# Cross-attention: Q and K pieces moved to the first visits, ctx in two halves, stack loads ahead of packing and stores, maxima three visits ahead

## The chip, the cores and the metric

The kernel runs on one core of a Trainium2 chip. TensorE multiplies into PSUM, VectorE (DVE), ScalarE (ACT) and GpSimd (POOL) compute, SyncE (SP) issues most DMAs; POOL and ACT issue some. The metric is the device time of one execution in microseconds, the lower the better. The three runs of the kernel before have a median of 2131.28 us (2120.72 to 2146.82).

## The reference

`x` is [8, 512, 320], the context [8, 1601, 512]; there are 20 heads of 16. The last 8 tokens of the context are four dummy and four image-prompt tokens with own weights and a mask from boxes; the first 1593 are text.

```python
q = split_heads(x @ w_q)                       # 20 heads of 16
k = split_heads(text @ w_k); v = split_heads(text @ w_v)
out_text = softmax(q k^T / 4) v
k_ip = split_heads(ip @ w_k_ip); v_ip = split_heads(ip @ w_v_ip)
out_ip = softmax(q k_ip^T / 4 + mask_ip) v_ip
out = (out_text + out_ip) @ w_out + b_out + x  # all in float32
```

## The kernel before

**Batches, groups, visits.** There are 8 batches of 5 groups; a group is four heads, so 40 groups run one after another. A group's scores are 12 tiles of 128 keys for each of four heads plus a half tile for two pairs: 50 exp tiles. They are taken in 17 **visits** (0 to 16) of three tiles (two in the last). In each visit TensorE multiplies three *max tiles* for a later group into the three banks of `max_bank` (`max_tile`, L602), three *exp tiles* of this group into `exp_bank` (`exp_tile`, L638, L642), at most one P·V tile (`pv_tile`, L654; visits 1, 5, 9 and 13 have none) and at most one *turn* of work from `work_plan`. ACT takes the exponentials (L815), VectorE the maxima of the three max banks in one reduction (L904).

**Maxima ahead.** A softmax needs the row maximum first. Round r of 17 reduces three banks; round 0 is the short tail of the keys (`max_rest`, 16 small matmuls, L613) and the first to touch the group's stack. `round_at` puts round v + LEAD in visit v, with LEAD = 2: in visit 15 starts round 0 of the group two after the one whose exps run, and the rounds of the next group end in visit 14. Then `negative_parts` on VectorE, a transposing matmul at visit NEG_AT = 15 (L536), a copy by ACT, and two DMAs from ACT's queue (L798) bring the negated maxima as extra rows into `q_stack`. The first exp tile of the next group waits for them (`neg_loaded`, L720).

**Stacks.** Scores run in float32r, on values split into a high and a low part. Projections K (`k_piece`, L480, two halves of four steps) and Q (`q_piece`, L491, three steps) go to `work_bank`; ACT copies them out, POOL splits them (`split_k`, `split_q`), SP stores them to scratch (`store_k`, `store_q`) and loads them back stacked (`load_k`, 12 DMAs, L364 and L367; `load_q`, 6 DMAs, L377) into a ring of three slots. Group n's stack comes from Q made in group n - 2 and K made in group n - 3.

**Other pieces.** V (`v_piece`, L513, L519; four steps, twelve tiles and a tail for each batch), OUT (`out_piece`, L529; the output projection of the batch before, four steps for each of four row tiles, in group 1), IP (the image tokens' scores), WA, WB, TA, TB (small). A piece is spread over visits by `put(group, piece, steps, (visit, steps), ...)`. `work_bank` is one bank, so a piece begins when the one before is copied out (`work_empty`). In group 2 VectorE does the mask softmax in visits 4 and 12.

**SP's order in a group.** `normalise` (sums, reciprocals, `r_wide`; L387 to L392) for the group before; in group 1 then `store_out` of the batch before (L405) and the pack; in others the pack (`o_sum` into `o_t`, four DMAs, L401); then `slot_free`, `load_k`, `store_q`, `load_q`; then `store_k`. In group 0 the residual `xres` (L437) is loaded first. ACT's `o_copy` in visit 0 waits for the pack before. POOL issues the next batch's ctx (`load_ctx`, L1082) behind the split of the last K piece of the batch.

Of the kernel before, what the change touches and what calls it, by code (L numbers as in the profile page):

```python
# [38 lines left out]
HEADS_IN_TURN = (0, 2, 1, 3)  # L39
# [11 lines left out]
LEAD = 2  # L51
# [9 lines left out]
V_EARLY = 8  # L61
PV_AT = {0: FULL, 2: 0, 3: 1, 4: 2, 6: 3, 7: 4, 8: 5, 10: 6, 11: 7, 12: 8, 14: 9, 15: 10, 16: 11}
NEG_AT = 15


def work_plan(first, last):
# [12 lines left out]
    put(0, ("V", 8), 4, (1, 4))  # L79
    put(0, ("V", 9), 4, (2, 2), (3, 2))  # L80
    put(0, ("V", 10), 4, (4, 2), (5, 2))
    put(0, ("V", 11), 4, (6, 2), (7, 2))
    put(0, ("V", 12), 4, (8, 1), (9, 3))
    put(0, ("K", 3, 0), 4, (10, 1), (11, 1), (12, 2))
    put(0, ("K", 3, 1), 4, (13, 3), (14, 1))
    put(0, ("IP", 2), 1, (16, 1))
    if not first:
        put(1, ("OUT", 0), 4, (0, 1), (1, 3))
        put(1, ("OUT", 1), 4, (2, 1), (3, 1), (4, 2))
        put(1, ("OUT", 2), 4, (5, 4))  # L90
        put(1, ("OUT", 3), 4, (6, 1), (7, 1), (8, 2))
    put(1, ("Q", 3), 3, (9, 3))
    put(1, ("K", 4, 0), 4, (10, 1), (11, 1), (12, 2))
    put(1, ("K", 4, 1), 4, (13, 3), (14, 1))
# [7 lines left out]
    if not last:  # L102
        put(2, ("V", 0), 4, (3, 1), (4, 1), (5, 2))
        put(2, ("K", 5, 0), 4, (6, 1), (7, 1), (8, 2))
        put(2, ("V", 1), 4, (9, 3), (10, 1))
        put(2, ("K", 5, 1), 4, (11, 1), (12, 1), (13, 2))
        put(3, ("Q", 5), 3, (0, 3))
        put(3, ("V", 2), 4, (1, 3), (2, 1))
        put(3, ("V", 3), 4, (3, 1), (4, 1), (5, 2))
        put(3, ("K", 6, 0), 4, (6, 1), (7, 1), (8, 2))  # L110
        put(3, ("V", 4), 4, (9, 3), (10, 1))
        put(3, ("K", 6, 1), 4, (11, 1), (12, 1), (13, 2))
        put(3, ("IP", 5), 1, (14, 1))
        put(4, ("Q", 6), 3, (0, 3))
        put(4, ("V", 5), 4, (1, 3), (2, 1))
        put(4, ("V", 6), 4, (3, 1), (4, 1), (5, 2))
        put(4, ("K", 7, 0), 4, (6, 1), (7, 1), (8, 2))
        put(4, ("V", 7), 4, (9, 3), (10, 1))
        put(4, ("K", 7, 1), 4, (11, 1), (12, 1), (13, 2))
        put(4, ("IP", 6), 1, (14, 1))  # L120
# [12 lines left out]
SCALE_AT = (1, 0, 1, 1, 1)  # L133
# [24 lines left out]
PRO_PLAN += [(("V", 6), ALL, 1), (("NEG", 0), ALL, 0), (("V", 7), ALL, 2)]  # L158
# [28 lines left out]
def cross_attention(nc, x, x_t, ctx_t, ctx_ip_t, boxes, grid, own_k_rows, own_v_rows, ident, w_q, w_k, w_v, w_k_ip, w_v_ip,  # L187
# [6 lines left out]
    with ctx:  # L194
# [142 lines left out]
        def _(sp):  # L337
# [94 lines left out]
            def body(b, first, last):  # L432
                number = lambda piece: work_number(b, piece, first, last)
                for g in range(NG):
                    group_no = b * NG + g
                    if g == 0 and not first:
                        sp.dma_start(xres[:, :, :], x[b - 1].rearrange("(t p) d -> p t d", p=128))\  # L437
                          .then_inc(residual_loaded, 16)
                    if group_no:
                        normalise(group_no - 1)  # L440
                    if g == 1:
                        if not first:
                            for t in range(QT):
                                store_out(b - 1, t, number(("OUT", t)))
                        pack(group_no - 1, 0, None if first else number(("OUT", QT - 1)))
                    elif group_no:
                        pack(group_no - 1, (g - 1) % NG, None)
# [5 lines left out]
                    if g == 2 and not first:  # L453
                        sp.wait_ge(out_stored, b * QT * 16)
                    if group_no + 3 < B * NG:
                        store_k(group_no + 3)

# [11 lines left out]
        def _(pe):  # L469
# [69 lines left out]
            def work(b, piece, turn, first, last):  # L539
# [12 lines left out]
                elif kind == "V":  # L552
                    if piece[1] == 0 and begins(turn):
                        pe.wait_ge(ctx_next_loaded, (b + 1) * CT * 16)
# [487 lines left out]
        def _(pool):  # L1042
# [37 lines left out]
            def load_ctx(b):  # L1080
                for c in range(CT):
                    pool.dma_start(ctxt[:, c, :], ctx_t[b, c * 128:(c + 1) * 128, :]).then_inc(ctx_next_loaded, 16)  # L1082
# [96 lines left out]
```

## Time and profile before

| | |
|---|---|
| median of three runs | 2131.28 us (2120.72 to 2146.82) |
| profiled execution | 2132.55 us, span 2130.7 us |
| mean granted TensorE clock | 0.952 |
| busy | PE 1921.7, DVE 1291.3, ACT 1203.1, POOL 301.9 us |
| maximum reductions (L904) | 672, 1726 ns each |
| chain that ended last | PE 60%, DVE 22%, DMA 9% |

The matmul rows overlap and their ends are modelled, so PE's busy share is not a measure of a full TensorE. In timeline rows the first number is the start, the second the duration; the bracket tells how long the engine had been idle before, and what ended that. One reduction L904 belongs to each visit, so the distance of their starts is the length of a visit.

### The profile page before, as it was taken

The numbers are of one execution on the slowest core, as the hardware profiler recorded it, in microseconds if no ns is written. First come the engines' busy times: TensorE is split into PE (matmuls) and PEld (weight loads), VectorE is DVE, ScalarE is ACT, GpSimd is POOL, SyncE is SP. The second block draws the span as 40 slices with busy tenths as digits, with TensorE's granted clock in tenths as the row PEclk, the third lists the DMA queues.
The fourth block names the chain that finished last, engine by engine and source line by source line (L and its number), as shares of the span: only waits on it lengthen the run. The fifth ranks groups of instructions, "written<-read, shape, count | busy, mean of one in ns | idle before, by whom it ended". The sixth has DMA issues, their size and how long they took to land.

```text
span 2130.7 us, 42231 instructions
## 1 busy us (share of the span) xinstructions
PE 1921.7 (90%) x17944; PEld 755.6 (35%) x17944; DVE 1291.3 (61%) x1025; ACT 1203.1 (56%) x2364; POOL 301.9 (14%) x356
## 2 busy tenths in 40 slices
PE   6888999979999799988999789998999989999777
PEld 2333333323333234333333333333333333343222
DVE  5665665646656566556666476565665656656650
ACT  0265666646655466555666466554665546665564
POOL 4001111121101111111110111102110121111000
PEclk9998999989999899999999899998999989999897
DMA  8405344254433533344333533335344253334201
GB/s 223 78 22 130 65 78 79 64 135 69 73 76 63 139 69 77 65 111 105 62 73 66 129 73 66 75 69 138 61 83 80 61 140 71 68 73 88 46 9 40
DMA packets 93229, 175.56 MB, mean 82 GB/s; under 512 B 37937, under 2 KB 62386, under 8 KB 89202
## 3 DMA queue, kind: packets, MB, share of 16 engines
q1 hardware_dynamic: 86066, 144.55, 34.5%
q0 software_dynamic: 5536, 27.67, 3.8%
q8 instruction: 141, 2.31, 0.5%
q10 hardware_dynamic: 1440, 0.66, 0.1%
q14 instruction: 46, 0.38, 0.1%
HBM read 117.75 MB, written 48.82 MB: 78 GB/s over the span
## 4 chain that ended last, share of the span: by engine, by line
PE 60%; DVE 22%; DMA 9%; SPq 4%; issue 3%; ACT 2%; ACTq 1%; POOLq 0%; POOL 0%
DVE tile_max L904 19%; PE max_bank L602 17%; PE pv_bank L654 14%; PE work_bank L480 7%; PE work_bank L513 7%; PE exp_bank L638 6%; DMA q_stack<-neg_rows 4%; PE work_bank L491 2%; PE work_bank L529 2%; DMA scratch_q<-q_parts 2%; DMA q_stack<-scratch_q 2%; PE max_bank L613 1%; ACT probs L815 1%; SPq L364 1%; SPq L367 1%
## 5 line engine op out<-in xcount | busy, mean ns | idle before, releaser
L904 DVE TENSOR_REDUCE tile_max<-max_bank 128x3 f32<-128x1536 f32 (+1 forms) x672 | 1159.6, 1726 | 726.0 <-PE max_bank L602 625.4
L815 ACT ACTIVATE probs<-exp_bank 128x512 f32<-128x512 f32 x1920 | 1007.7, 598 | 560.6 <-PE exp_bank L638 559.1
L602 PE MATMUL max_bank<-k_stack,q_stack 48*128 48x512 f32 x1896 | 471.6, 471 | 97.4 <-DVE tile_max L904 82.3
L654 PE MATMUL pv_bank<-probs,v_ones 128*17 128x512 f32 x3840 | 536.7, 622 | 0.0
L638 PE MATMUL exp_bank<-q_stack,k_stack 50*128 50x512 f32 x1920 | 425.3, 410 | 28.2 <-DMA q_stack<-neg_rows 26.8
L602 PEld LDWEIGHTS max_bank<-k_stack,q_stack 48*128 48x128 f32 x1896 | 191.2, 188 | 488.2 <-DVE tile_max L904 446.7
L638 PEld LDWEIGHTS exp_bank<-q_stack,k_stack 50*128 50x128 f32 x1920 | 244.5, 190 | 98.3 <-DMA q_stack<-neg_rows 35.4
L480 PE MATMUL work_bank<-ctxt,wk 128*32 128x400 f32 x2560 | 262.2, 513 | 14.3 <-DMA ctxt<-in_ctx_t 11.2
L513 PE MATMUL work_bank<-wv,ctxt 128*32 128x320 f32 x3072 | 247.6, 438 | 0.8 <-ACT vip L755 0.5
L1049 POOL TENSOR_TENSOR k_parts<-k_full,zero 128x400 fp32r<-128x400 f32 x80 | 68.2, 852 | 759.8 <-ACT k_full L755 754.7
L513 PEld LDWEIGHTS work_bank<-wv,ctxt 128*32 128x32 f32 x3072 | 91.3, 110 | 155.0 <-issue 86.8
L480 PEld LDWEIGHTS work_bank<-ctxt,wk 128*32 128x32 f32 x2560 | 79.8, 112 | 183.7 <-issue 171.4
L654 PEld LDWEIGHTS pv_bank<-probs,v_ones 128*17 128x17 f32 x3840 | 72.2, 96 | 168.2 <-issue 165.9
L1078 POOL TENSOR_TENSOR o_sum<-o_sum,r_wide 128x512 f32<-128x512 f32 x40 | 51.8, 1294 | 564.3 <-DMA r_wide<-scratch_r 564.3
L815 ACT ACTIVATE probs_tail<-exp_bank 128x512 f32<-128x512 f32 x80 | 43.4, 594 | 92.2 <-PE exp_bank L642 92.1
L613 PE MATMUL max_bank<-k_stack,q_stack 48*128 48x64 f32 x640 | 50.7, 288 | 49.5 <-DMA q_stack<-scratch_q 49.5
L1057 POOL TENSOR_TENSOR q_parts<-q_full,zero 128x256 fp32r<-128x256 f32 x40 | 24.5, 612 | 479.6 <-ACT q_full L755 479.5
L1052 POOL TENSOR_TENSOR k_parts<-k_full,k_parts 128x400 fp32r<-128x400 f32 x80 | 83.4, 1042 | 6.3
L755 ACT ACTIVATE k_full<-work_bank 128x400 f32<-128x400 f32 x80 | 40.4, 506 | 77.5 <-PE work_bank L480 75.5
L755 ACT ACTIVATE v_ones<-work_bank 128x320 f32<-128x320 f32 (+1 forms) x112 | 47.4, 423 | 55.9 <-PE work_bank L513 52.5
L529 PE MATMUL work_bank<-wout,o_t 128*32 128x320 f32 (+1 forms) x928 | 75.4, 436 | 0.0
L491 PE MATMUL work_bank<-xt,wq 128*32 128x256 f32 x960 | 69.3, 428 | 1.2 <-ACT k_full L755 1.2
(90 smaller groups left out, 675.5 us busy)
## 6 DMA issues: line engine op xcount, KB each, us to landing
k_stack<-scratch_k SPq DMA_DIRECT2D x240, 200.0 KB, 6.0
scratch_k<-k_parts SPq DMA_DIRECT2D x80, 400.0 KB, 4.7
ctxt<-in_ctx_t POOLq DMA_DIRECT2D x28, 800.0 KB, 9.5
q_stack<-scratch_q SPq DMA_DIRECT2D x240, 64.0 KB, 2.3
scratch_q<-q_parts SPq DMA_DIRECT2D x80, 128.0 KB, 6.6
r_wide<-scratch_r SPq DMA_DIRECT2D x40, 256.0 KB
o_t<-o_sum SPq DMA_DIRECT2D x160, 32.0 KB, 2.0
xres<-in_x SPq DMA_DIRECT2D x8, 640.0 KB, 6.7
```

The costliest lines, as they stand in the source:

```text
L480: last = nc.tensor.matmul(work_bank[half * GR + at:half * GR + at + rows, 0:CHUNK], wk[:, ct, dims:dims + rows], ctxt[:, ct, keys:keys + C ...
L491: last = nc.tensor.matmul(work_bank[half * GR + at:half * GR + at + rows, 0:QHALF], wq[:, ct, dims:dims + rows], xt[:, ct, half * QHALF:(h ...
L513: last = nc.tensor.matmul(work_bank[at:at + rows, 0:D], ctxt[:, ct, key:key + rows], wv[:, ct, :], start=(ct == 0), stop=(ct == CT - 1))
L529: last = nc.tensor.matmul(bank[at:at + rows, :], o_t[0:deep, k, t * 128 + at:t * 128 + at + rows], wout[0:deep, k, :], start=(k == 0), sto ...
L602: nc.tensor.matmul(round_place(n, r)[:, k, :], exact(q_stack[stack, slot, c, t * 128:(t + 1) * 128]), exact(k_stack[stack, slot, c, chunk ...
L613: mm = nc.tensor.matmul(max_bank[:, side, at * TAIL:(at + 1) * TAIL], exact(q_stack[stack, slot, c, t * 128:(t + 1) * 128]), exact(k_stack ...
L638: nc.tensor.matmul(bank[:, :], exact(k_stack[stack, slot, c, kt * 128:(kt + 1) * 128]), exact(q_stack[stack, slot, c, :]), start=True, sto ...
L654: last = nc.tensor.matmul(pv_bank[h * 32:h * 32 + VW, :], v_ones[:, v_slot(b, kt), head * VW:(head + 1) * VW], p, start=(kt == 0), stop=(k ...
L755: return nc.scalar.activation(dst, src, ACT.Copy)
L815: nc.scalar.activation(dst, exp_bank[:, at % BANKS, :], ACT.Exp, scale=SCALE).then_inc(probs_ready, 1)
L904: nc.vector.reduce_max(out_at, scores, AX.X).then_inc(max_taken, 1)
L1052: nc.gpsimd.tensor_tensor(exact(part[:, 1, :]), k_full[:, c, :], part[:, 0, :], ALU.subtract).then_inc(k_split, 1)
```

## The change

- `LEAD` is 3: rounds of maxima run one visit earlier against the exps; `NEG_AT` is 14. `HEADS_IN_TURN` swaps the two sides of the array, so that a visit's exp tiles still start on the other side than its max tiles end. `PRO_PLAN` gains V 8 with one more round; `V_EARLY` is 9, so V 8 is made a batch ahead.
- `work_plan`: in groups 0 and 1 the Q and K pieces come in visits 0 to 5; V and OUT follow. The pieces of groups 2 to 4 shift likewise, V 8 now ending group 4.
- SP: the stack loads come ahead of the pack; in group 1 the pack waits for OUT 3 and comes ahead of the four stores; the wait for stored outputs moves to the next batch's `xres` load.
- POOL: ctx is loaded in two halves of eight DMAs in all, one behind the split of each half of K 4; `scale_o` of groups 0 and 1 comes behind the first K half.

```diff
--- before.py
+++ after.py
@@ -36,7 +36,7 @@
 ROWS = STACK + PARTS
 SIDES = 2
 SIDE = 128 // SIDES
-HEADS_IN_TURN = (0, 2, 1, 3)
+HEADS_IN_TURN = (2, 0, 3, 1)
 RING = 3
 EXPS = FULL * GH + GH // 2
 BLOCKS = (0, 0, 1)
@@ -48,7 +48,7 @@
 BANKS = 3
 VISITS = FULL * GH // BANKS + 1
 ROUNDS = VISITS
-LEAD = 2
+LEAD = 3
 CHUNKS = FULL // 4
 WIDE = 512
 PAIRS = GH // SIDES * QT
@@ -58,9 +58,9 @@
 SCALE = float(DH) ** -0.5
 NEG = -10000.0
 GRID_W, GRID_H = 32, 16
-V_EARLY = 8
+V_EARLY = 9
 PV_AT = {0: FULL, 2: 0, 3: 1, 4: 2, 6: 3, 7: 4, 8: 5, 10: 6, 11: 7, 12: 8, 14: 9, 15: 10, 16: 11}
-NEG_AT = 15
+NEG_AT = 14
 
 
 def work_plan(first, last):
@@ -76,22 +76,21 @@
         assert at == total
 
     put(0, ("Q", 2), 3, (0, 3))
-    put(0, ("V", 8), 4, (1, 4))
-    put(0, ("V", 9), 4, (2, 2), (3, 2))
-    put(0, ("V", 10), 4, (4, 2), (5, 2))
-    put(0, ("V", 11), 4, (6, 2), (7, 2))
-    put(0, ("V", 12), 4, (8, 1), (9, 3))
-    put(0, ("K", 3, 0), 4, (10, 1), (11, 1), (12, 2))
-    put(0, ("K", 3, 1), 4, (13, 3), (14, 1))
+    put(0, ("K", 3, 0), 4, (1, 3), (2, 1))
+    put(0, ("K", 3, 1), 4, (3, 1), (4, 1), (5, 2))
+    put(0, ("V", 9), 4, (6, 1), (7, 1), (8, 2))
+    put(0, ("V", 10), 4, (9, 3), (10, 1))
+    put(0, ("V", 11), 4, (11, 2), (12, 2))
+    put(0, ("V", 12), 4, (13, 4))
     put(0, ("IP", 2), 1, (16, 1))
+    put(1, ("Q", 3), 3, (0, 3))
+    put(1, ("K", 4, 0), 4, (1, 3), (2, 1))
+    put(1, ("K", 4, 1), 4, (3, 1), (4, 1), (5, 2))
     if not first:
-        put(1, ("OUT", 0), 4, (0, 1), (1, 3))
-        put(1, ("OUT", 1), 4, (2, 1), (3, 1), (4, 2))
-        put(1, ("OUT", 2), 4, (5, 4))
-        put(1, ("OUT", 3), 4, (6, 1), (7, 1), (8, 2))
-    put(1, ("Q", 3), 3, (9, 3))
-    put(1, ("K", 4, 0), 4, (10, 1), (11, 1), (12, 2))
-    put(1, ("K", 4, 1), 4, (13, 3), (14, 1))
+        put(1, ("OUT", 0), 4, (6, 2), (7, 2))
+        put(1, ("OUT", 1), 4, (8, 1), (9, 3))
+        put(1, ("OUT", 2), 4, (10, 2), (11, 2))
+        put(1, ("OUT", 3), 4, (12, 1), (13, 3))
     put(1, ("IP", 3), 1, (16, 1))
     put(2, ("Q", 4), 3, (0, 3))
     put(2, ("IP", 4), 1, (1, 1))
@@ -100,23 +99,24 @@
     put(3, ("TA",), 4, (16, 4))
     put(4, ("TB",), 4, (16, 4))
     if not last:
-        put(2, ("V", 0), 4, (3, 1), (4, 1), (5, 2))
-        put(2, ("K", 5, 0), 4, (6, 1), (7, 1), (8, 2))
-        put(2, ("V", 1), 4, (9, 3), (10, 1))
-        put(2, ("K", 5, 1), 4, (11, 1), (12, 1), (13, 2))
+        put(2, ("V", 0), 4, (2, 1), (3, 1), (4, 2))
+        put(2, ("K", 5, 0), 4, (5, 2), (6, 1), (7, 1))
+        put(2, ("V", 1), 4, (8, 1), (9, 3))
+        put(2, ("K", 5, 1), 4, (10, 1), (11, 1), (12, 2))
+        put(2, ("V", 2), 4, (13, 4))
         put(3, ("Q", 5), 3, (0, 3))
-        put(3, ("V", 2), 4, (1, 3), (2, 1))
-        put(3, ("V", 3), 4, (3, 1), (4, 1), (5, 2))
-        put(3, ("K", 6, 0), 4, (6, 1), (7, 1), (8, 2))
-        put(3, ("V", 4), 4, (9, 3), (10, 1))
-        put(3, ("K", 6, 1), 4, (11, 1), (12, 1), (13, 2))
+        put(3, ("V", 3), 4, (1, 3), (2, 1))
+        put(3, ("K", 6, 0), 4, (3, 1), (4, 1), (5, 2))
+        put(3, ("V", 4), 4, (6, 1), (7, 1), (8, 2))
+        put(3, ("K", 6, 1), 4, (9, 3), (10, 1))
+        put(3, ("V", 5), 4, (11, 1), (12, 1), (13, 2))
         put(3, ("IP", 5), 1, (14, 1))
         put(4, ("Q", 6), 3, (0, 3))
-        put(4, ("V", 5), 4, (1, 3), (2, 1))
-        put(4, ("V", 6), 4, (3, 1), (4, 1), (5, 2))
-        put(4, ("K", 7, 0), 4, (6, 1), (7, 1), (8, 2))
-        put(4, ("V", 7), 4, (9, 3), (10, 1))
-        put(4, ("K", 7, 1), 4, (11, 1), (12, 1), (13, 2))
+        put(4, ("V", 6), 4, (1, 3), (2, 1))
+        put(4, ("K", 7, 0), 4, (3, 1), (4, 1), (5, 2))
+        put(4, ("V", 7), 4, (6, 1), (7, 1), (8, 2))
+        put(4, ("K", 7, 1), 4, (9, 3), (10, 1))
+        put(4, ("V", 8), 4, (11, 1), (12, 1), (13, 2))
         put(4, ("IP", 6), 1, (14, 1))
     return plan
 
@@ -130,7 +130,7 @@
 
 
 SPLITS = tuple((("Q", g + 2), ("K", g + 3, 0), ("K", g + 3, 1)) for g in range(NG))
-SCALE_AT = (1, 0, 1, 1, 1)
+SCALE_AT = (2, 2, 1, 1, 1)
 INVERT_AT = 2
 
 
@@ -155,7 +155,7 @@
 PRO_PLAN += [(("Q", 0), (0, 3, 3), 0), (("KIP",), ALL, 0), (("IP", 0), ALL, 0), (("K", 1, 0), ALL, 0), (("K", 1, 1), ALL, 0)]
 PRO_PLAN += [(("Q", 1), (0, 3, 3), 0), (("IP", 1), ALL, 0), (("VIP",), ALL, 0)]
 PRO_PLAN += [(p, half, 1) for p in [("V", t) for t in range(4)] + [("K", 2, 0), ("K", 2, 1), ("V", 4), ("V", 5)] for half in HALVES]
-PRO_PLAN += [(("V", 6), ALL, 1), (("NEG", 0), ALL, 0), (("V", 7), ALL, 2)]
+PRO_PLAN += [(("V", 6), ALL, 1), (("NEG", 0), ALL, 0), (("V", 7), ALL, 2), (("V", 8), ALL, 1)]
 assert sum(n for _, _, n in PRO_PLAN) == ROUNDS + LEAD
 PRO = [piece for piece, turn, _ in PRO_PLAN if begins(turn)]
 PRO_ORDER = {p: n for n, p in enumerate(PRO)}
@@ -434,26 +434,26 @@
                 for g in range(NG):
                     group_no = b * NG + g
                     if g == 0 and not first:
+                        if b > 1:
+                            sp.wait_ge(out_stored, (b - 1) * QT * 16)
                         sp.dma_start(xres[:, :, :], x[b - 1].rearrange("(t p) d -> p t d", p=128))\
                           .then_inc(residual_loaded, 16)
                     if group_no:
                         normalise(group_no - 1)
-                    if g == 1:
-                        if not first:
-                            for t in range(QT):
-                                store_out(b - 1, t, number(("OUT", t)))
-                        pack(group_no - 1, 0, None if first else number(("OUT", QT - 1)))
-                    elif group_no:
-                        pack(group_no - 1, (g - 1) % NG, None)
                     if group_no + 2 < B * NG:
                         slot_free(group_no + 2)
                         load_k(group_no + 2)
                         store_q(group_no + 2)
                         load_q(group_no + 2)
-                    if g == 2 and not first:
-                        sp.wait_ge(out_stored, b * QT * 16)
+                    if group_no and g != 1:
+                        pack(group_no - 1, (g - 1) % NG, None)
                     if group_no + 3 < B * NG:
                         store_k(group_no + 3)
+                    if g == 1:
+                        pack(group_no - 1, 0, None if first else number(("OUT", QT - 1)))
+                        if not first:
+                            for t in range(QT):
+                                store_out(b - 1, t, number(("OUT", t)))
 
             batches(body)
             end = len(PRO) + FIRST_WORK + (B - 2) * LOOP_WORK + len(work_order(False, True))
@@ -551,7 +551,7 @@
                     ip_piece(piece[1], number(("Q", piece[1])), b + (2 if piece[1] >= NG else 1))
                 elif kind == "V":
                     if piece[1] == 0 and begins(turn):
-                        pe.wait_ge(ctx_next_loaded, (b + 1) * CT * 16)
+                        pe.wait_ge(ctx_next_loaded, (b + 1) * 2 * CT * 16)
                     v_piece(piece[1], range(turn[0], turn[1]))
                 elif kind == "OUT":
                     if piece[1] == 0 and begins(turn):
@@ -1077,9 +1077,10 @@
                 pool.wait_ge(r_wide_loaded, (group_no + 1) * 16)
                 nc.gpsimd.tensor_tensor(o_sum[:, :], o_sum[:, :], r_wide[:, :], ALU.mult).then_inc(o_scaled, 1)
 
-            def load_ctx(b):
-                for c in range(CT):
-                    pool.dma_start(ctxt[:, c, :], ctx_t[b, c * 128:(c + 1) * 128, :]).then_inc(ctx_next_loaded, 16)
+            def load_ctx(b, c):
+                for ct in range(CT):
+                    chunk = lambda a: a.rearrange("p (f c n) -> p f c n", f=2, c=2)[:, :, c, :]
+                    pool.dma_start(chunk(ctxt[:, ct, :]), chunk(ctx_t[b, ct * 128:(ct + 1) * 128, :])).then_inc(ctx_next_loaded, 16)
 
             def load_x(b):
                 pool.dma_start(xt[:, 0:2, :], x_t[b, 0:256, :].rearrange("(c p) n -> p c n", p=128)).then_inc(x_next_loaded, 16)
@@ -1114,8 +1115,8 @@
                             scale_o(b * NG + g - 1)
                         if piece[0] == "K":
                             split_k(b * NG + piece[1], piece[2], number(piece))
-                            if piece == ("K", 4, 1) and not last:
-                                load_ctx(b + 1)
+                            if piece[1] == NG - 1 and not last:
+                                load_ctx(b + 1, piece[2])
                         else:
                             split_q(b * NG + piece[1], number(piece))
                             if piece == ("Q", 4) and not last:
```

## Rows read from the trace of the kernel before

**Rows 1.** The page's first line: the span.

```profile
span 2130.7 us, 42231 instructions
```

**Rows 2.** Waits of TensorE: line, releaser, us in total, times, longest.

```profile
PE max_bank L602 <- DVE tile_max L904: 82.3, 89, 4.1
PE max_bank L613 <- DMA q_stack<-scratch_q: 49.5, 7, 10.5
PE exp_bank L638 <- DMA q_stack<-neg_rows: 26.8, 18, 5.6
```

**Rows 3.** Timeline of VectorE: reduction of visit 0, second and last batch.

```profile
341.46 1.76 DVE L904 TENSOR_REDUCE tile_max<-max_bank 128x3 f32<-128x1536 f32 x1 [1.41 <-PE max_bank L602]
...
1871.45 1.76 DVE L904 TENSOR_REDUCE tile_max<-max_bank 128x3 f32<-128x1536 f32 x1 [1.41 <-PE max_bank L602]
```

**Rows 4.** Timeline of VectorE, fourth batch: reductions behind visits of different work.

```profile
863.84 1.76 DVE L904 TENSOR_REDUCE tile_max<-max_bank 128x3 f32<-128x1536 f32 x1 [1.44 <-PE max_bank L602]
...
869.75 1.76 DVE L904 TENSOR_REDUCE tile_max<-max_bank 128x3 f32<-128x1536 f32 x1 [1.20 <-PE max_bank L602]
...
889.02 1.76 DVE L904 TENSOR_REDUCE tile_max<-max_bank 128x3 f32<-128x1536 f32 x1 [0.82 <-PE max_bank L602]
...
897.89 1.76 DVE L904 TENSOR_REDUCE tile_max<-max_bank 128x3 f32<-128x1536 f32 x1 [1.30 <-PE max_bank L602]
...
901.26 1.23 DVE L904 TENSOR_REDUCE tile_max<-max_bank 128x16 f32<-128x1024 f32 x1 [0.94 <-PE max_bank L613]
903.30 1.76 DVE L904 TENSOR_REDUCE tile_max<-max_bank 128x3 f32<-128x1536 f32 x1 [0.82 <-PE max_bank L602]
...
977.06 0.81 DVE L928 TENSOR_TENSOR s_ip<-s_ip,mask 128x640 f32<-128x640 f32 x1
...
979.50 1.75 DVE L904 TENSOR_REDUCE tile_max<-max_bank 128x3 f32<-128x1536 f32 x1
...
1018.34 1.76 DVE L904 TENSOR_REDUCE tile_max<-max_bank 128x3 f32<-128x1536 f32 x1 [1.42 <-PE max_bank L602]
```

**Rows 5.** Timeline around the wait of L613, second batch, group 1.

```profile
427.94 1.32 SPq L348 DMA_DIRECT2D scratch_q<-q_parts  x2
...
436.60 2.63 SPq L377 DMA_DIRECT2D q_stack<-scratch_q  x6
...
437.79 2.16 POOL L1082 DMA_DIRECT2D ctxt<-in_ctx_t  x4
...
445.34 1.92 PE L613 MATMUL max_bank<-k_stack,q_stack 48*128 48x64 f32 x16 [9.44 <-DMA q_stack<-scratch_q]
```

**Rows 6.** Timeline where the fourth batch begins: neg rows and the residual.

```profile
848.38 1.23 DVE L904 TENSOR_REDUCE tile_max<-max_bank 128x16 f32<-128x1024 f32 x1 [0.33 <-PE max_bank L613]
848.39 1.38 SPq L437 DMA_DIRECT2D xres<-in_x  x1
...
849.01 2.53 ACTq L798 DMA_DIRECT2D q_stack<-neg_rows  x2
...
855.33 0.95 PE L638 MATMUL exp_bank<-q_stack,k_stack 50*128 50x512 f32 x3 [1.77 <-DMA q_stack<-neg_rows]
...
860.65 1.76 DVE L904 TENSOR_REDUCE tile_max<-max_bank 128x3 f32<-128x1536 f32 x1 [5.30 <-PE max_bank L602]
```

**Rows 7.** Timeline of SP, third batch, group 1: the output stores.

```profile
662.21 15.68 SPq L405 DMA_DIRECT2D out<-xres  x4
```

**Rows 8.** Windows over groups 1 of six batches: first, sum. PEclk follows POOL.

```profile
393.60:455.30 61.70, 51.04 (x456) 20.37 (x455) 32.42 (x28) 28.33 (x55) 9.11 (x13) 0.87 0.47 123
...
sum 356.20, PE 303.06 PEld 120.25 DVE 194.51 ACT 169.98 POOL 54.69; mean PE 50.51 PEld 20.04 DVE 32.42 ACT 28.33 POOL 9.11
```

**Rows 9.** Timeline of VectorE, first batch, group 2.

```profile
203.99 1.76 DVE L904 TENSOR_REDUCE tile_max<-max_bank 128x3 f32<-128x1536 f32 x1 [10.53 <-PE max_bank L602]
```

**Rows 10.** DMA issues: count, KB each, median us from issue to landing.

```profile
ctxt<-in_ctx_t POOLq DMA_DIRECT2D x28, 800.0 KB, 9.5
...
ctxt<-in_ctx_t SPq DMA_DIRECT2D x8, 400.0 KB, 7.9
```

## The prediction, made before the changed kernel had run

> **What bounds the kernel now.** I began with the page: a span of 2130.7 us [rows 1]; the profiled execution took 2132.55 us, 1.3 us above the median of 2131.28. The sum below is made against it. TensorE is busy most of the span, but its ends are modelled, so I read its waits next [rows 2]: 82.3 us for a maximum reduction on VectorE, 49.5 us in seven waits of the tail maxima (L613) for `q_stack<-scratch_q`, 26.8 us in 18 waits of the first exp tile for `q_stack<-neg_rows`.
>
> To price visits I then read the starts of VectorE's reductions L904, one for each visit [rows 3, 4]. In a light visit a reduction of 1.76 us is followed by 0.82 us of idle, in which TensorE refills the one max bank: 2.58 us, a floor that no visit with three max tiles passes. More work on TensorE shows as a longer idle before the next reduction; 1.76 plus that idle is the visit. Four V steps without a P·V tile: 3.20. Two V steps with one: 2.96. Three K steps without: 3.06. Three Q steps with: 3.18. One K step with: 2.58. All fit one rule: 1.05 for the six score matmuls, 0.85 for P·V, and per step 0.53 (V, and OUT of the same shape), 0.67 (K), 0.43 (Q), or the floor if that is larger. So one V or K step with P·V, and two K steps without, hide under the floor; three V or OUT without P·V are 2.65.
>
> A batch in the middle costs (1871.45 - 341.46) / 6 = 255.0 us [rows 3]; 17 floors in each of five groups would be 219. The rest is stalls and visits above the floor.
>
> **The stalls of a batch.** (a) Group 1. SP issues everything of a group in one order. Here it spends 15.68 us in four output stores, each waiting for its OUT piece [rows 7], then packs, loads K, stores and loads q. The q loads go out at 436.60, 8.7 us after their store; the POOL queue starts the ctx load at 437.79 beside them, and L613 starts only at 445.34, after 9.44 us of idle [rows 5]. The granted clock over such a group is 0.87 of full [rows 8]: behind the stall part of it ran at 1.2 GHz and not 2.4. The six groups 1 in the middle last 356.2 us, 59.4 each; by the rule above their plan costs 46.7. Lost: 12.6, of which 1.0 is for neg rows. (b) Before group 0 the tail reduction starts at 848.38, the neg rows go out at 849.01 beside the xres load, and the first exp tile starts at 855.33, having waited 1.77. The next reduction comes 5.30 + 1.76 = 7.06 after its predecessor, where a Q visit is 3.18: 3.9 lost, the clock included [rows 6]. (c) Groups 3 and 4 run without stall, 45.75 each; what is left for group 2 is 255.0 - 52.6 - 59.4 - 91.5 = 51.5, by the rule 49.1: 2.4 lost. Together 19.0; without stalls today's batch is 236.0.
>
> **What the change does to them.** *Stack loads first.* In group 1 SP is free 9 us into the group (where the first store stands now, 662.21 with the group's first exp at 653.2). Q of that stack is now made in visit 0, K was stored a group before. Twelve K loads (6 us), q stores (1.3), their landing (8), q loads (2.6), landing (6.1, the one seen beside a ctx load [rows 5]): all in at 33. With three visits of lead it is needed in visit 14, 38.6 us in. (a) goes, with 5 us to spare. *Neg rows.* From the start of the tail reduction they are usable 855.33 - 848.38 = 6.95 later [rows 6]. Visit 0 now comes one visit later behind that reduction: 2.05 + 2.58 + 2.58 less 0.3 = 6.9 before groups 1 and 2, 7.5 to 8.2 before the others, whose last visit is longer. The slow landing of 6.95 had xres beside it; SP now reaches that load earlier, since the last K piece of group 4 ends in visit 10, not 13. I take no wait.
>
> *What is late next.* The pack in group 1: OUT 3 ends in visit 13, 39.7 in; four issues of 2.5 us together and 2 us of landing: 44.2. Behind it in SP stand the stores and the next group's sums. ACT needs the pack for its copy of o_sum at 49.2. Nobody waits.
>
> *The ctx halves.* Eight transfers for four: some 2 us more of issue on POOL, which is idle there; the load of K's second half is behind them by that much. They start in visits 3 and 6 of group 1 and are needed in visit 2 of group 2, over 30 us later. Pieces of 400 KB landed in 7.9 us, of 800 KB in 9.5 [rows 10]: between nothing, if they overlap, and 8 x 7.9 - 4 x 9.5 = 25 us more. Both ends fit, so I take nothing.
>
> **The repacking**, by the rule. Visits 0 to 12. Group 0: 3.18, 3.06, six floors, 2.96, 2.65, 2.58, 2.96, 2.96 = 35.8. Group 1: 3.18, 3.06, four floors, 2.96, 2.96, 2.58, 2.65, 2.96, 2.96, 2.58 = 36.2. Group 2: 3.18, three floors, 4.12 for the mask softmax on VectorE (979.50 less the reduction that ends at its start, 977.06 + 0.08 - 1.76) [rows 4], four floors, 2.65, two floors, 3.95 for its second part, the same pattern with smaller operations = 37.1. Groups 3 and 4: 3.18, 2.65, six floors, 2.96, 3.06, three floors = 35.1 each. Visit 13 now leads from the last full reduction to the tail one. Today that is 901.26 - 897.89 = 3.37 with P·V and one K step, which leaves 1.85 for exp tiles, tail matmuls and latency. Four V steps then make 3.98 (group 0), three OUT 3.45 (group 1), two V the floor of that pair, 3.0 (groups 3, 4); in group 2 VectorE's delay absorbs part, 3.3. Visit 14: 903.30 - 901.26 = 2.05, with WA 2.35, with IP 2.2 (estimates: the added matmuls beyond VectorE's time). Visit 15 a floor; visit 16 as today, 2.58, 2.58, 3.5, 3.18, 3.18. Sums: 47.0 + 46.9 + 48.8 + 46.0 + 46.0 = 234.7. The repacking itself gives 1.3; a batch gains 255.0 - 234.7 = 20.3, six of them 122.
>
> First batch: no OUT, but a stall of 10.53 before the second reduction of group 2 [rows 9], 9 of it lost, and a little repacking: -11. Last batch: three quarters of a middle one, -14, as its groups 2 to 4 have little to repack. Prologue: V 8 and a twentieth reduction come ahead of batch 0: between a floor, +2.6, and four V steps at the low clock behind the sparse prologue plus a reduction, +6; nearer the second, +5.
>
> Sum: 2132.55 - 122 - 11 - 14 + 5 = 1990.6. **Forecast 1990 us.**
>
> **Rivals.** 1. *The neg rows stay late* (10%). For: 6.95 against a cover of 6.9 before groups 1 and 2 leaves nothing when a K store runs beside. Against: xres was beside that one, and is not there. If each batch keeps the 3.9 and 1.0 it loses now: 1990 + 7.5 x 4.9 = 2027.
>
> 2. *Stack 3 is late still* (5%). For: the ctx halves now run beside its K and q transfers. Against: it needs over 5 us more than computed. If (a) and (c) returned whole: 1990 + 7 x 15.0 = 2095, within 2% of now. The Trainium skill, "DMA: Bandwidth & Descriptors", Anatomy of one DMA, charges each transfer from POOL 2.0 us plus its bytes at 436 GB/s, which speaks against the split: four more transfers are 8 us more, an estimate from that page. If all of that delayed the q loads, the stall would be 3 us a batch and the time 2011. The two landings of [rows 10] do grow less than in proportion to size, as the rule wants, but each is over twice what it gives.
>
> 3. *The pack behind OUT 3* (3%), which ends slower. SP stands in group 1 before the pack; ACT's copy of o_sum, and behind it every exp tile, waits for it. It decides from 5 us of lateness. For a time slower by 2%, 2174, it must cost 184 / 8 = 23 us a batch, so the pack must land 28 us later than computed. Only OUT sliding out of its group would do that.
>
> 4. *The clock falls in light visits* (2%, 2090 at worst). In group 1 of batch 0, with no OUT, reductions were up to 3.4 us apart now. The new plan leaves few visits without work.
>
> **How the numbers follow.** The forecast's case has 0.80 and by itself a range of 1972 to 2010: prologue 3 us either way, neg rows late by 1 us at up to 16 boundaries, repacking wrong by 0.2 us in 40 groups. With rival 1 the range for 8 in 10 is 1970 to 2035. Faster by over 2% (below 2089, about what repeated runs, 2120.72 to 2146.82 here, can tell from no change): 0.91. Within 2%, rival 2 mostly: 0.05. Slower: 0.04.
>
> **What would show it.** Right: no wait of L613 for `scratch_q` in group 1; under 5 us in all of exp tiles for neg rows; middle batches of 234 to 236 us between reductions; granted clock near 0.99; the q loads of group 1 issued before its output stores. Wrong: a middle batch of 240 or more, a wait of ACT for the pack, VectorE idle over 1.5 us in visit 0, or reductions over 2.6 us apart in visits with one K step and P·V, which are only 0.01 under the floor.

## The result, and the profile after

| | before | changed |
|---|---|---|
| median | 2127.79 us of 4 runs | 2053.22 us of 4 runs (2051.17 to 2058.60) |
| profiled execution | 2132.55 us | 2051.17 us, span 2049.3 us |
| mean granted clock | 0.952 | 0.960 |

The ratio is 0.964, 95% interval 0.957 to 0.971: faster by 3.6%, 81 us between the two profiled executions. Forecast were 1990 us and a range that ended at 2035. The gain is little over half of the forecast, and the direction alone was right.

TensorE's waits in the changed kernel (line, releaser, us in total, times, longest), to be held against [rows 2]:

```profile
PE max_bank L613 <- DMA q_stack<-scratch_q: 21.3, 7, 4.6
...
PE exp_bank L638 <- ACT probs L815: 3.3, 7, 0.5
```

No wait for neg rows is left (26.8 us before). The wait of the tail maxima for `q_stack<-scratch_q` is still there, seven times, 21.3 us for 49.5. The middle of the kernel by the reductions of visit 0 in the second and the last batch (timeline of VectorE):

```profile
345.32 1.76 DVE L904 TENSOR_REDUCE tile_max<-max_bank 128x3 f32<-128x1536 f32 x1 [1.41 <-PE max_bank L602]
...
1802.53 1.76 DVE L904 TENSOR_REDUCE tile_max<-max_bank 128x3 f32<-128x1536 f32 x1 [1.40 <-PE max_bank L602]
```

(1802.53 - 345.32) / 6 = 242.9 us a batch, against 255.0 before [rows 3] and 234.7 forecast; the prediction had named 240 or more as a sign of being wrong. The windows over groups 1 of the six middle batches say where the 8.2 us are:

```profile
633.00:689.50 56.50, 51.89 (x454) 20.48 (x452) 32.30 (x28) 28.43 (x55) 12.66 (x17) 0.88 0.60 127
...
sum 328.40, PE 307.74 PEld 122.07 DVE 193.79 ACT 170.59 POOL 76.04; mean PE 51.29 PEld 20.35 DVE 32.30 ACT 28.43 POOL 12.67
```

328.4 / 6 = 54.7 where the ledger had 46.9 (59.4 before, [rows 8]), and the clock of the group shown is 0.88. The wait of L613 is 3.0 us of these 7.8 (21.3 in seven groups). The rest is TensorE behind it at the lower of its two levels, 1.2 GHz for 2.4: the granted clock was 0.54 in the stretch from 675 to 690 us, and visits 14 to 16 of the six groups last 3.2, 3.6 and 4.2 us on average for 2.05, 2.58 and 2.58. The other four groups came out close to the forecast: 47.1, 49.2, 45.9 and 45.9 for 47.0, 48.8, 46.0 and 46.0, by the distances of the reductions. Now group 1 of the third batch, which begins at 633.0: SP's and POOL's issues and the wait (start, duration):

```profile
643.62 2.91 POOL L1083 DMA_DIRECT2D ctxt<-in_ctx_t  x4
...
649.26 1.29 SPq L348 DMA_DIRECT2D scratch_q<-q_parts  x2
...
654.82 2.90 POOL L1083 DMA_DIRECT2D ctxt<-in_ctx_t  x4
...
671.49 2.64 SPq L377 DMA_DIRECT2D q_stack<-scratch_q  x6
...
676.09 1.92 PE L613 MATMUL max_bank<-k_stack,q_stack 48*128 48x64 f32 x16 [4.31 <-DMA q_stack<-scratch_q]
```

SP issued the q store 16.3 us in, 1 us later than forecast. The q loads, which wait for it, left 38.5 us in, when the stack was already due, and not 24 us in. The chain of waits has the reason in one piece:

```profile
649.93 21.55 DMA scratch_q<-q_parts
```

A store of 256 KB in two DMAs took 21.55 us to land. It stands in SP's queue behind `r_wide` and twelve K loads, and the two ctx halves of 1.6 MB each start 5.6 us before it and 5.6 us behind it. The last batch loads no ctx; there the same store took 12 us, the q loads left 28.7 us in, and nothing waited.

### The profile page after: what moved, and what is told of

Its sections match the earlier page's. It is cut to its first block, busy times and chain, and to the rows that moved or that the text cites. A ratio compares the mean times of both kernels' runs of the same rounds, so it can differ in the third digit from the quotient of the medians.

```text
span 2049.3 us, 42245 instructions
## 1 busy us (share of the span) xinstructions
PE 1916.1 (93%) x17944; PEld 760.7 (37%) x17944; DVE 1295.4 (63%) x1025; ACT 1205.1 (59%) x2364; POOL 328.2 (16%) x384
## 4 chain that ended last, share of the span: by engine, by line
PE 60%; DVE 24%; DMA 8%; issue 4%; SPq 3%; ACT 0%; POOLq 0%; POOL 0%
DVE tile_max L904 20%; PE max_bank L602 18%; PE pv_bank L654 13%; PE work_bank L480 7%; DMA scratch_q<-q_parts 7%; PE work_bank L513 7%; PE exp_bank L638 5%; PE work_bank L491 3%; PE max_bank L613 2%; PE exp_bank L642 1%; SPq L364 1%; SPq L367 1%; PE work_bank L519 1%; DMA q_stack<-scratch_q 1%; SPq L377 1%
## 5 line engine op out<-in xcount | busy, mean ns | idle before, releaser
L638 PE MATMUL exp_bank<-q_stack,k_stack 50*128 50x512 f32 x1920 | 435.4, 408 | 3.3 <-ACT probs L815 3.3
L638 PEld LDWEIGHTS exp_bank<-q_stack,k_stack 50*128 50x128 f32 x1920 | 255.1, 191 | 71.1 <-ACT probs L815 32.6
L480 PE MATMUL work_bank<-ctxt,wk 128*32 128x400 f32 x2560 | 257.3, 509 | 14.3 <-DMA ctxt<-in_ctx_t 11.2
L513 PE MATMUL work_bank<-wv,ctxt 128*32 128x320 f32 x3072 | 254.8, 442 | 0.8 <-ACT vip L755 0.5
L755 ACT ACTIVATE v_ones<-work_bank 128x320 f32<-128x320 f32 (+1 forms) x112 | 47.1, 420 | 85.1 <-PE work_bank L513 77.4
L613 PE MATMUL max_bank<-k_stack,q_stack 48*128 48x64 f32 x640 | 50.3, 292 | 23.4 <-DMA q_stack<-scratch_q 21.3
L491 PE MATMUL work_bank<-xt,wq 128*32 128x256 f32 x960 | 60.4, 385 | 1.2 <-ACT k_full L755 1.2
```

The source lines that it names most:

```text
L480: last = nc.tensor.matmul(work_bank[half * GR + at:half * GR + at + rows, 0:CHUNK], wk[:, ct, dims:dims + rows], ctxt[:, ct, keys:keys + C ...
L491: last = nc.tensor.matmul(work_bank[half * GR + at:half * GR + at + rows, 0:QHALF], wq[:, ct, dims:dims + rows], xt[:, ct, half * QHALF:(h ...
L513: last = nc.tensor.matmul(work_bank[at:at + rows, 0:D], ctxt[:, ct, key:key + rows], wv[:, ct, :], start=(ct == 0), stop=(ct == CT - 1))
L613: mm = nc.tensor.matmul(max_bank[:, side, at * TAIL:(at + 1) * TAIL], exact(q_stack[stack, slot, c, t * 128:(t + 1) * 128]), exact(k_stack ...
L638: nc.tensor.matmul(bank[:, :], exact(k_stack[stack, slot, c, kt * 128:(kt + 1) * 128]), exact(q_stack[stack, slot, c, :]), start=True, sto ...
L755: return nc.scalar.activation(dst, src, ACT.Copy)
```

## The experiments

Three theories at first. **Q**: all transfers of group 1 share DMA engines that are full, and the early ctx halves stand in the way; what counts is when they run. **S**: pieces of 400 KB are what costs. **P**: the new order on SP itself is what costs, with or without ctx. Each kernel below is the changed kernel with the edit shown, unless it says otherwise; ratios are to the kernel before. Where "the third batch" is named, rows and distances are of that batch alone.

| run | edit | median us | ratio, interval | group 1 | L613 for q, L638 for neg rows (us in all) |
|---|---|---|---|---|---|
| before | | 2126 to 2131 | | 59.3 | 49.5, 26.8 |
| changed | | 2053.2 | 0.964, 0.957 to 0.971 | 54.8 | 21.3, 0 |
| e1 | q store first | 2030.9 | 0.952, 0.944 to 0.961 | 52.4 | 14.8, 0 |
| e2 | ctx behind stack 3 | 2010.8 | 0.944, 0.938 to 0.951 | 46.9 | 0, 6.5 |
| e3 | ctx whole, behind K 4,1 | 1998.1 | 0.938, 0.931 to 0.945 | 47.0 | 0, 0 |
| e4 | ctx in eight, behind K 4,1 | 2000.5 | 0.939, 0.933 to 0.946 | 47.1 | 1.6, 0 |
| e5 | second half left out | 2003.0 | 0.944, 0.940 to 0.949 | 47.8 | 1.3, 0 |
| e6 | e3 with LEAD 2 | 1994.9 | 0.938, 0.934 to 0.941 | 46.5 | 0, 0 |
| e7 | before, SP order alone | 2089.8 | 0.983, 0.980 to 0.987 | 47.7 | 0, 58.3 |
| e8 | e3, prologue interleaved | 1997.6 | 0.940, 0.938 to 0.943 | 47.9 | 3.3, 0 |
| e9 | changed with LEAD 2 | 2017.6 | 0.947, 0.944 to 0.950 | 50.1 | 10.8, 0.5 |
| e10 | e7 with LEAD 3 | 2076.0 | 0.977, 0.972 to 0.981 | 47.4 | 2.4, 21.3 |
| e11 | e6, group 2 rearranged | 1985.0 | 0.932, 0.930 to 0.935 | 46.5 | 0.8, 0 |

(Group 1: mean of the middle six, by the reductions' starts.)

**e1, the q store ahead of the K loads.**

```diff
-                        load_k(group_no + 2)
                         store_q(group_no + 2)
+                        load_k(group_no + 2)
                         load_q(group_no + 2)
```

> The changed kernel, but SP stores q before it issues the twelve loads of K, in every group. In the changed kernel the q store of group 1 lands 21.5 us after its issue, and stack 3 is late by about 8 us a batch. Theory Q (order in one queue plus shared engines): the q store stands behind r_wide and the K loads, which share the 16 DMA engines with the first ctx half. Then a q store ahead of the K loads lands in 8 us or less in group 1, the q loads go out by 20 us into the group, the wait of L613 for scratch_q falls from 21.3 to under 5 us, and the time is 1995 to 2010. Theory S (the ctx load in pieces of 400 KB is slow itself and whatever runs beside it is held up): the order does not matter, the K loads are held up as long, and the time stays within 2040 to 2055.

2030.9 us, between both. In the third batch, whose group 1 begins at 628.5, the q loads did leave 21.5 us in:

```profile
650.02 3.23 SPq L377 DMA_DIRECT2D q_stack<-scratch_q  x6
```

The store left 6 us earlier and was there 11 us after its issue, for 22 in the changed kernel, so its place behind the K loads was half of its delay. But the q loads now stand behind the K loads themselves. They took 7.3 us to land in the median of all groups (2.3 in the changed kernel), and in this group 17.8, with the DMA share at 0.97 to 1.11 from 643.5 to 663.5. The stack was in at 42.2 us for 43.1, and L613 waited 14.8 us in all. Order alone moves the waiting, and theory Q's number was too hopeful.

**e2, ctx behind stack 3.**

```diff
-                            if piece[1] == NG - 1 and not last:
-                                load_ctx(b + 1, piece[2])
+                            if piece == ("K", NG - 1, 1) and not last:
+                                pool.wait_ge(stack_loaded[(b * NG + 3) % RING], loads_of(b * NG + 3))
+                                load_ctx(b + 1, 0)
+                                load_ctx(b + 1, 1)
```

> The changed kernel, but both ctx halves are issued only behind the split of the last K piece and once all loads of stack 3 have landed. Theories Q and S both expect the stall of group 1 gone (no wait of L613 for scratch_q, the q store landing in about 11 us as in the groups without a ctx load) and a time of 1992 to 2000, which is the ledger of the prediction with its rival 2 taken out. A third theory, P (the stall is from the new order on SP itself, not from ctx): the stall stays, 2045 to 2055.

The stall of group 1 is gone, every middle group 1 at 46.9 us: theory P falls. The time is 11 us over the expectation, and that is a second collision:

```profile
658.15 5.79 POOL L1083 DMA_DIRECT2D ctxt<-in_ctx_t  x8 [10.01 <-DMA q_stack<-scratch_q]
...
665.38 1.32 ACTq L798 DMA_DIRECT2D q_stack<-neg_rows  x2
...
673.28 0.73 PE L638 MATMUL exp_bank<-q_stack,k_stack 50*128 50x512 f32 x3 [1.42 <-DMA q_stack<-neg_rows]
```

The late ctx load runs while the neg rows of 16 KB travel; the exp tile that needs them starts 7.9 us after their issue. Group 2 is 51.4 us on average in the middle batches, for 49.2 in the changed kernel.

**e3 and e4, the moment without and with the new shape.** e3 puts the old whole load back, four DMAs of 800 KB; e4 keeps the eight of 400 KB. Both stand behind the split of K 4,1, 23 to 25 us into the group. (Excerpt: in e3 the old body of `load_ctx` and the old count of TensorE's wait for it are back too.)

```diff
-                            if piece[1] == NG - 1 and not last:
-                                load_ctx(b + 1, piece[2])
+                            if piece == ("K", NG - 1, 1) and not last:
+                                load_ctx(b + 1)        # e4: load_ctx(b + 1, 0); load_ctx(b + 1, 1)
```

> The changed kernel with one part undone: ctx is loaded whole, four transfers of 800 KB behind the split of the last K piece, about 22 us into group 1. Q: only the end of the q store (landing about 28 us in) and the q loads meet it; they land at 33 to 38 us, needed at 38.6; time 1993 to 2010. S: the same or better, 1993 to 2000. P: 2045 to 2055.

> The changed kernel with eight transfers of 400 KB as now, but all issued behind the split of the last K piece, as the whole load would be. This takes the moment from the shape. Q: as with the whole load, within 0.5% of it. S: the shape is what costs, so a stall of several us a batch stays: 2030 to 2055.

1998.1 and 2000.5 us. The same eight transfers, moved from 11 and 22 us into the group to 23 us and later, give back 53 us, and at that moment four or eight transfers make no difference that can be told: theory S falls, the moment decides. (Four whole transfers at the early moment were not run.) SP's timeline of e3 in group 1 of the third batch, which begins at 618.6:

```profile
634.39 1.27 SPq L348 DMA_DIRECT2D scratch_q<-q_parts  x2
...
647.51 2.80 SPq L377 DMA_DIRECT2D q_stack<-scratch_q  x5
```

The loads leave 13 us behind the store for 22, 28.9 us into the group. By then ctx is under way too (issue at 641.78). It met less: the DMA share was 0.59 from 638.6 to 643.6, where the changed kernel, in the 10 us behind the store's issue, had 1.04 and 1.12. And K loads took at most 10.0 us to land in e3, 16.7 in the changed kernel.

**e5, half the bytes.** (Excerpt: TensorE's wait for ctx counts four transfers for eight too.)

```diff
-                            if piece[1] == NG - 1 and not last:
-                                load_ctx(b + 1, piece[2])
+                            if piece == ("K", NG - 1, 0) and not last:
+                                load_ctx(b + 1, 0)
```

> The changed kernel with the second half of every later ctx load left out (its keys keep the first batch's values): 1.6 MB beside the K and q transfers of group 1 instead of 3.2 MB, at the same early moment. Theory B (bytes: the stack is late because all transfers of group 1 share engines that are full, so it lands when most bytes have gone through): the q store lands in about 14 us instead of 21.5, the wait of L613 is gone, time 1995 to 2003. Theory M (the moment: any ctx load that starts together with the K loads holds the q store up): a wait of several us stays, 2020 to 2045.

2003.0 us; one of its four executions took 2024.4, at a mean granted clock of 0.965 for 0.978. In the third batch, whose group 1 begins at 623.6, the q loads leave 17.7 us behind the store's issue:

```profile
640.02 1.27 SPq L348 DMA_DIRECT2D scratch_q<-q_parts  x2
657.75 2.64 SPq L377 DMA_DIRECT2D q_stack<-scratch_q  x6
```

The time is at the edge of theory B's range and far from M's; the landing lies between the two. On average over the middle batches the first half at the early moment costs the store 5.4 us of landing (e3 to e5) and the second half another 3.1 (e5 to the changed kernel), and only with both is the stack late everywhere. The q loads leave 34 us in here, and the six of them need 4.6 us from the first issue to the last landing (671.49 to 676.05 in the changed kernel), against a need at 38.6: of the 5 us to spare that I had forecast nothing is left. L613 waited 1.3 us in three batches, and behind one of these waits the clock fell (0.67 from 1603.8 to 1612.0), for 4.9 us in all.

**e6, the third visit of lead taken out of e3**: `LEAD` 2, `NEG_AT` 15, `HEADS_IN_TURN` (0, 2, 1, 3), V 8 with no round in the prologue.

> The kernel with the whole ctx load behind the last K piece (1998 us), with LEAD 2, the tail round and neg rows one visit later, the old order of heads, and V 8 in the prologue without a round. It prices the third visit of lead. Theory N (the lead is what hides the neg rows, at the price of before): waits of L638 for neg rows come back at 3.9 us before each batch and 1.0 before groups 1 and 2, 1998 + 7.5 x 5.9 - 3 = 2039. Theory X (most of the 3.9 came from the xres load beside the neg rows, which now goes out earlier): landings of 5.2 us against covers of 4.3 and 4.9 leave about 1.0 before groups 1 and 2 and 0.3 before the others, 2.9 us a batch, less about 4 in the prologue: 2012 to 2020.

1994.9 us, and no wait for neg rows at all: N is refuted, and X too had them too late. Where nothing large is beside them they arrive in time for an exp tile that starts 3.6 us after their issue (third batch, before group 2; the same interval in [rows 6] was 6.3, with the xres load issued 0.6 us and two K stores issued 1.9 us ahead of them):

```profile
654.87 1.30 ACTq L798 DMA_DIRECT2D q_stack<-neg_rows  x2
...
658.44 0.64 PE L638 MATMUL exp_bank<-q_stack,k_stack 50*128 50x512 f32 x3
```

**e7, the kernel before with SP's order alone.**

```diff
                     if group_no:
                         normalise(group_no - 1)
+                    if group_no + 2 < B * NG:
+                        slot_free(group_no + 2)
+                        load_k(group_no + 2)
+                        store_q(group_no + 2)
+                        load_q(group_no + 2)
                     if g == 1:
                         ...          # stores and pack, as before
-                    if group_no + 2 < B * NG:
-                        ...          # the same four calls
```

> The kernel before with one part of the change alone: SP issues the stack loads ahead of stores and pack; the work plan, the lead and ctx stay. Theory G (the SP order alone takes the stall of group 1 away and nothing comes for it): q loads out by 38 us into group 1, needed 43.6 in; 2127 - 7 x 12 = 2043. Theory V (the wait moves: without the stall the neg rows of group 2 leave beside the ctx load, as they did in batch 0, where they landed in 8.8 us and about 9 us were lost): no wait of L613, but seven waits of L638 of 4 to 6 us before group 2, and 2090 to 2105.

2089.8 us, the lower end of theory V's range. L613 waits no more and group 1 is 47.7 us; the wait is now 58.3 us on neg rows in 23 waits, and group 2 begins with 10.7 to 12.5 us from reduction to reduction in the middle batches. Third batch, timeline:

```profile
686.53 1.30 ACTq L798 DMA_DIRECT2D q_stack<-neg_rows  x2
...
686.89 2.16 POOL L1082 DMA_DIRECT2D ctxt<-in_ctx_t  x4
...
695.85 1.22 PE L638 MATMUL exp_bank<-q_stack,k_stack 50*128 50x512 f32 x3 [5.43 <-DMA q_stack<-neg_rows]
```

Neg rows and ctx leave within 0.4 us, and the exp tile that waits for the rows starts 9.3 us after their issue. So SP's order alone takes away the stall of group 1 and is not enough for the time.

**e10, e7 with the third visit of lead** (and K 3,1 and K 4,1 with all four steps in visit 13, so that the neg piece may stand in visit 14).

> The kernel before with the stack loads first on SP (2090 us, where the neg rows wait) and the third visit of lead added; K 3,1 and K 4,1 take all four steps in visit 13, so that the neg piece can stand in visit 14; the prologue gets one more round. Work plan and ctx stay otherwise. Theory L (the lead is a cure for neg rows that leave beside a large load, as these do): waits of L638 fall from 58 us to under 8, 2090 - 8 x 12 + 15 for the longer visit 13 = 2005 to 2020. Theory O (the ctx load still meets them, now issued within a microsecond of them, and the landing takes as long as the cover): 2040 or more.

2076.0 us, as theory O had it. The lead cured the boundaries without ctx: visit 0 of group 0 went from 7.0 us in e7 (median of the middle batches) to 3.18, that of group 1 from 3.62 to 2.58. Before group 2 ctx still leaves within 0.4 us of the neg rows; they land later than the lead covers by 3 us (21.3 us in seven waits), and with the clock that falls behind (0.69 from 685 to 696 us) it is 8.2 to 10.0 us from reduction to reduction.

**e9, the changed kernel with LEAD 2** (the edit of e6 on it).

> The changed kernel with LEAD 2 alone undone (neg rows a visit later, old order of heads, V 8 in the prologue without a round); ctx stays in early halves. Theory H (harm: here the third visit of lead hides nothing, since the neg rows need under 3.6 us where no load is beside them, and it moves the deadline of stack 3 one visit forward): the wait of L613 shrinks by about 3 us a batch and the prologue by 5: 2015 to 2030. Theory N (the lead does hide the neg rows): waits of L638 return and the time is 2053 or more.

2017.6 us, as theory H says: 36 us faster than the changed kernel. The stack is due a visit later, so the same late q loads cost 10.8 us of waiting for 21.3, and the exp tiles waited for neg rows once, 0.5 us. In this plan the third visit of lead hides next to nothing and costs a deadline.

**e8 and e11, versions to beat both.** e8 cuts V 7 and V 8 of e3's prologue in halves between the rounds.

> The kernel with the whole ctx load behind the last K piece (1998 us), with V 7 and V 8 of the prologue cut in halves with one round behind each of the first three halves. In the changed kernel VectorE stood idle 5.96 us before the tail round of group 1, while TensorE ran V 7 whole at the low clock. The first exp tile should start 2 to 3 us earlier, everything behind it unchanged: 1995 us, 1993 to 1998. If the neg rows of group 0 set that start, nothing is gained: 1998.

1997.6 us, no gain. The first exp tile started at 93.8 us for 97.8 in e3, but group 1 of the first and of the fourth batch then stalled (3.3 us of waits in the two, and granted clocks of 0.50 and 0.61 behind them): they last 53.3 and 52.0 us for 48.4 and 46.9. That took it back. e11 changes e6:

```diff
-    put(2, ("IP", 4), 1, (1, 1))
+    put(2, ("IP", 4), 1, (4, 1))
-        put(2, ("V", 0), 4, (2, 1), (3, 1), (4, 2))
+        put(2, ("V", 0), 4, (1, 2), (2, 1), (3, 1))
-                        if (g, v) == (2, 4):    # mask softmax
+                        if (g, v) == (2, 5):
```

> The kernel with whole ctx load and LEAD 2 (1994.9 us), with the image piece of group 2 moved from visit 1 to visit 4, V 0 to visits 1 to 3, and the mask softmax one visit later. In the kernel it starts from, the light visit 1 of group 2 is followed by a visit 2 of 3.96 us in which the matmuls ran at 1.2 GHz, in six batches, and visit 4 is not covered by work. Theory C (the clock fell for want of work): visit 2 returns to 2.58 and one step over the floor goes: 1995 - 6 x 1.4 - 8 x 0.4 = 1980 to 1987. Theory K (it falls wherever that moment is): 1990 to 1996.

1985.0 us, the fastest, as theory C had it: visit 2 of group 2 is 2.58 us for 3.9 to 4.0 in e6, where the granted clock was 0.57 from 664 to 668 us. The three edits were not tested apart, and the executions of e6 and e11 overlap at their ends (1987.6 to 1998.4 and 1982.9 to 1990.4 us). The ratio of e11 to the kernel before is 0.932, that is 6.8% faster.

## Why the prediction was wrong

**What bounds it, and the price of a visit**: right. The rule from six kinds of visit gave groups 0, 2, 3 and 4 within 0.4 us each, and group 1 where it does not stall (46.9 us in e2, 47.0 in e3, forecast 46.9). The floor of 2.58 us held, and so did visit 13 of group 0 (4.01 us, forecast 3.98). One term was missed: visits 12 and 13 of group 2, 7.6 us for 7.25. POOL's split of K 5,1 fell on VectorE's softmax (last section).

**The step that failed** is the landing of the q store in "stack loads first", taken as 8 us behind twelve K loads. It took 21.5, so the stack was in at about 43 us and not 33, against a need at 38.6. Of the 61 us between forecast and measurement in the profiled executions, the six middle batches make 8.2 x 6 = 49, all of it in group 1 but 0.4 a batch. The first batch makes 7.6, for the same reason, since its group 1 took 55.0; the prologue was 7.2 us longer and not 5; and the last batch gained 12.5 and not 14. The 8 us were read from a store behind the same K loads [rows 5], but one without the two things that the change put beside it. The first is `r_wide`, which now stands directly ahead of the K loads: in groups without ctx the store lands in 11 to 12 us, and in e7, which changes SP's order alone, it lands in 11 in group 0, for 6 before. The second is ctx, which makes it 20 in group 1 on average. And I let ctx and stack overlap after finding that they start in the same visits: rival 2 was the mechanism, with 5% for a whole return of the stall. It came in part, 8 of 15 us a batch, and of the 8 only 3.0 are the wait; the rest is mostly the low clock behind it. Where rival 2 counts a stall of 3 us a batch it counts 3 us of time for it, and such a stall cost 7.8 here.

**The halves at nothing** was the wrong way round. I had looked at when ctx is needed (late, true), not at whom it meets. e3 and e4 show that the early moment costs 53 to 55 us here and the shape, at the late moment, nothing that can be told (1998.1 and 2000.5 us). So the rule of the Trainium skill on the price of a transfer decides nothing here; the one that bears on it is in the same page of the Trainium skill, "DMA: Bandwidth & Descriptors", Issuing engines are not separate DMA queues: transfers issued from different engines run on the same 16 DMA engines and interleave. The trace agrees: the store issued by SP took 21.55 us beside POOL's ctx load, 11 to 12 without it.

**The neg rows**: right that no wait is left, wrong in the reason. I credited the third visit of lead, from a landing of 6.95 us. That landing had company: the xres load was issued 0.6 us [rows 6] and K stores 1.9 us ahead of the neg rows. In e6, the new plan without the lead and with ctx late, both are issued 5.5 us or more ahead of them, and nothing waits. That it is this distance, and no other part of the plan, is read from the timelines and was not tested by itself. In the old plan the lead does count (e10, visit 0 of group 0), where the neg rows meet these transfers.

**The pack behind OUT 3**: right, nobody waited for it, though it came later than I said where the stack was late (issued 42.5 us in, not 39.7, and 5.7 us long).

**The clock**: 0.960 and not 0.99. Most of the difference follows the stall: the mean is 0.974 to 0.983 in e2 to e6, e8 and e11, where the stall is gone or small. No kernel reached 0.99, so that sign was set too high.

What each part is worth, by runs: SP's order alone 38 us and a wait moved on (e7); the whole change with ctx whole at its old place in the plan, behind K 4,1, 128 us together (e3); the early halves -55; the third visit of lead about nothing (1998.1 us in e3, 1994.9 in e6) or -36 (the changed kernel against e9). The remaining 8 us between e3 and the forecast are in the middle batches, 0.8 us each and nearly all of it in group 2, and 2 us each in the first and the last batch; the prologue was 4.2 us longer, less than the 5 allowed. What of them is due to chance from run to run stays open: the first reduction of the first batch came at 97.7 to 101.5 us in the six kernels with the same prologue (the changed one and e1 to e5).

## What to carry to other kernels

Before you call a transfer free because its result is needed late, list the transfers that it meets, and how long each may take; the small ones on which an engine waits (here 256 KB and 16 KB) pay for the large one. Take landing times from a stretch where the queue is as full as it will be, not from the median of the page. And when a stall is removed, look at which waits come next in that stretch: here the same ctx load hit the q store, the neg rows or nobody, by 10 us of difference in its start.

## What the runs showed of the hardware

K loads, each into 16 partitions, fill the DMA engines at a low rate. Two windows (last two columns: DMA share, GB/s): K loads with no large transfer beside them, in group 3 of the third batch of the kernel before, and K loads beside ctx, in group 1 of the changed kernel:

```profile
780.00:785.00 5.00, 5.00 (x48) 1.89 (x48) 3.38 (x2) 3.15 (x6) 0.00 (x0) 1.00 0.83 137
```

```profile
647.50:652.50 5.00, 4.87 (x52) 1.82 (x44) 2.97 (x3) 3.12 (x7) 0.83 (x1) 1.00 1.04 144
```

The engines are busy nearly throughout at 137 GB/s (the first load left at 780.3), and the ctx load beside them adds little: from 645 to 660 us the changed kernel moved 130, 157 and 171 GB/s in 5 us each, at shares of 0.98 to 1.12. The ctx load of the kernel before, with little beside it, moved more than twice that at the same share (its window):

```profile
440.00:445.00 5.00, 0.00 (x0) 0.00 (x0) 0.00 (x0) 0.00 (x0) 0.57 (x2) 0.50 0.98 313
```

So the share tells that a stretch is full, the rate does not. Whether it is the 16 partitions that make the K loads slow was not tested.

And VectorE and POOL held each other up. In group 2 of the changed kernel the product of two SBUF tiles took 1.50 us in all seven batches where POOL splits a K piece beside it, and 0.82 in the last, where it does not; it took 0.82 or 0.83 in all eight batches of the kernel before. POOL's subtraction, which started inside it, took 1.50 or 1.51 in the same seven, where its mean was 1.04 on the page of before:

```profile
725.90 1.50 DVE L943 TENSOR_TENSOR p_ip<-s_ip,ip_max 128x640 f32<-128x640 f32 x1
```

```profile
726.80 1.51 POOL L1052 TENSOR_TENSOR k_parts<-k_full,k_parts 128x400 fp32r<-128x400 f32 x1
```
